# Hybrid attention and FFN kernel: the next set's row pairs in the FFN down stages turned by VectorE blocks and device memory in place of TensorE

## The reference

```python
x = x + attn_a(layernorm(x), ...)          # chunked linear attention with decay, 4 heads, chunk 128
x = x + ffn(layernorm(x), wq_gate, s_gate, wq_up, s_up, wq_down, s_down)
x = x + attn_b(layernorm(x), W_q, W_k, W_v, W_o)   # softmax attention over 1024 tokens, 1 head
x = x + ffn(layernorm(x), ...)             # the same FFN weights
# ffn: W = (wq - 128) * s[:, None];  ffn(x) = W_down(silu(W_gate x) * (W_up x)),  hidden width 1408
```

## Time and profile before

| | us |
|---|---|
| median of 3 runs | 955.58 (955.57 to 955.67) |
| the profiled execution, first to last instruction | 954.9 |

### The profile page before, as it was taken

How to read it: one execution, slowest core, us unless ns; L and a number is a source line. 1 busy time by engine, 2 the same in 40 slices (tenths; PEclk the granted TensorE clock), 3 DMA queues, 4 the chain that set the end, 5 groups by cost and what they waited for, 6 DMA issues and landing times.

```text
span 954.9 us, 13285 instructions
## 1 busy us (share of the span) xinstructions
PE 941.6 (99%) x4744; PEld 534.5 (56%) x4744; DVE 608.9 (64%) x1128; ACT 460.8 (48%) x918; POOL 478.6 (50%) x487
## 2 busy tenths in 40 slices
PE   7999999999999999999999999999999999999998
PEld 4888988888744454444544455445455444544443
DVE  7555657849677586776855466445465676766543
ACT  4443334356577545664533455323454665456631
POOL 5433424477266676666840043304333566665575
PEclk9999999999999999999999999999999999999999
DMA  9401300024200000000000000000000000110001
GB/s 324 165 11 34 133 23 23 2 89 142 95 29 1 1 1 1 1 1 1 1 1 1 1 1 1 1 1 1 1 0 1 1 0 1 45 45 1 1 23 67
DMA packets 14738, 30.31 MB, mean 32 GB/s; under 512 B 2064, under 2 KB 2128, under 8 KB 14672
## 3 DMA queue, kind: packets, MB, share of 16 engines
q1 hardware_dynamic: 14672, 29.45, 8.6%
HBM read 25.22 MB, written 4.23 MB: 31 GB/s over the span
## 4 chain that ended last, share of the span: by engine, by line
PE 93%; ACT 1%; DVE 1%; POOL 1%; DMA 1%; SPq 1%; issue 0%; POOLq 0%; DVEq 0%
PE psum L2078 54%; PE psum L2325 14%; PE psum L2327 14%; PE psum L2453 7%; PE psum L2127 2%; PE psum L2464 1%; DMA bq_col<-bq 1%; PE psum L2212 1%; PE psum L2116 1%; ACT probs L1329 0%; DVE xb_lo L1983 0%; SPq L658 0%; ACT xb_hi L1335 0%; POOL wvT_lo L922 0%; POOL wo_lo L925 0%
## 5 line engine op out<-in xcount | busy, mean ns | idle before, releaser
L872 POOL TENSOR_TENSOR hid<-hid,hid_hi 128x512 f32<-128x512 f32 x88 | 102.7, 1167 | 101.6 <-DVE hid_hi L1777 101.6
L2325 PE MATMUL psum<-xf,w_gu 128*128 128x512 f16 x352 | 133.8, 380 | 0.0
L2325 PE MATMUL psum<-xf,w_s 128*128 128x512 f16 x264 | 100.0, 379 | 0.6 <-DVE up L1750 0.4
L2327 PE MATMUL psum<-xf,w_gu 128*128 128x512 f16 x264 | 100.1, 379 | 0.0
L1191 ACT ACTIVATE hid_lo<-hid 128x512 f16<-128x512 f32 x88 | 55.0, 625 | 33.0 <-POOL hid L872 33.0
L868 POOL TENSOR_TENSOR hid<-up,gate 128x512 f32<-128x512 f32 x44 | 56.0, 1273 | 23.8 <-ACT gate L1186 23.8
L2327 PE MATMUL psum<-xq,w_s 128*128 128x512 f16 x176 | 66.7, 379 | 0.0
L2325 PEld LDWEIGHTS psum<-xf,w_gu 128*128 128x128 f16 x352 | 34.3, 98 | 53.9 <-ACT acc L1176 15.5
L1186 ACT ACTIVATE gate<-gate,sg_xs 128x512 f32<-128x512 f32 x44 | 31.7, 721 | 65.7 <-DVE gate L1760 65.7
L734 POOL TENSOR_TENSOR xrstd<-xvar,minus_half 128x1 f32<-128x1 f32 x48 | 25.5, 548 | 59.2 <-DVE xvar L1448 59.2
L1777 DVE TENSOR_SCALAR hid_hi<-hid 128x512 f16<-128x512 f32 x88 | 39.1, 444 | 19.4 <-POOL hid L868 17.9
(11 more groups left out here) (308 smaller groups left out, 2560.1 us busy)
## 6 DMA issues: line engine op xcount, KB each, us to landing
cla_wide<-cla_dram SPq DMA_DIRECT2D x16, 256.0 KB, 3.3
out<-xres SPq DMA_DIRECT2D x16, 256.0 KB, 2.0
xres<-x SPq DMA_DIRECT2D x3, 1024.0 KB, 13.3
codes_gu<-gateT SPq DMA_DIRECT2D x1, 2816.0 KB, 11.5
codes_gu<-upT SPq DMA_DIRECT2D x1, 2816.0 KB, 10.7
codes_da<-downT SPq DMA_DIRECT2D x1, 1536.0 KB, 6.8
codes_db<-downT SPq DMA_DIRECT2D x1, 1280.0 KB, 11.2
xres<-x SPq DMA_DIRECT2D x4, 256.0 KB, 3.2
```

Source lines behind the costliest of these rows:

```text
L872: nc.gpsimd.tensor_tensor(hid[:, :], hid[:, :], hid_part(hid_hi, j, half), ALU.subtract).then_inc(rest_done, 1)
L2325: nc.tensor.matmul(bank(use[0]), w, x_operand(piece, k, False), start=start and k == 0, stop=False, skip_group_check=not start)
L2327: last = nc.tensor.matmul(bank(use[0]), w, x_operand(piece, k, True), start=False, stop=k == 1, skip_group_check=not start)
```

## The change

In the down stages of blocks 0, 1 and 2 TensorE no longer turns the pairs. DVE normalises a pair into `xn` (even i) or a second buffer (odd i) and turns it in place in 32x32 blocks with one `transpose` of 128x1024 (`x_blocks`). SP writes the pair to a new device-memory tensor `blocks` by four transfers, one for each group of 32 partitions, and loads it by four more into `turned[i % 2]` in SBUF with the blocks at their turned places; each transfer consists of 1024 runs of 128 bytes. A load of pair i waits for its store, and for pairs 2 and 3 for the readers of pair i-2. ACT and POOL read `turned` in place of PSUM and `x_first`; the four copies to x_first (line 996) go. DVE's x_second reads `turned` too. `X_AFTER` becomes (3, 4, 5, 6). x_blocks of pairs 0 and 1 stand ahead of down tile 0 on DVE, those of pairs 2 and 3 after tiles 2 and 3 (`BLOCKS_AFTER`), pair 3 thus behind x_second of pair 0. In block 2 SP's stores of finished rows stand between its transfers of blocks. Banks 0, 1, 3 and 4 lose two uses each in the three stages. The turns of sets F0, B1 and F2 stay on TensorE.

```diff
--- before.py
+++ after.py
@@ -46,7 +46,13 @@
 
 X_STATS = {(0, 2): ((0,), (1,), (2, 3)), (0, 3): ((4,), (5,), (6, 7))}
 
-X_AFTER = (1, 3, 5, 6)
+X_AFTER = (3, 4, 5, 6)
+
+BLOCKS_AFTER = {2: 2, 3: 3}
+
+SQ = 32
+QUADS = P // SQ
+TURN_DMAS = 16 * QUADS
 
 
 HS = 2.0 ** -18
...
@@ -203,6 +210,9 @@
     x_last = [at(f"x_last{v}", X_TEMPS[v][2], D) for v in range(4)]
     X_PLACE = (0, 1, 1, 2, 3, 1)
 
+    xn_pair = [xn, at("xn_pair1", Z + 77824, 2 * D)]
+    turned = [at(f"turned{i}", Z + 61440 + 4096 * i, 2 * D) for i in range(2)]
+
 
     w_s = at("w_s", Z + 104448, 6 * HID, F16)
     wd_a = at("wd_a", Z + 121344, 5 * D, BF16)
@@ -254,6 +264,8 @@
 
 
     cla_dram = nc.dram_tensor("cla_dram", [4 * 4 * HEADS, P], F32, kind="Internal").ap()
+
+    blocks = nc.dram_tensor("blocks", [4 * len(MOVED), QUADS, 2 * KT, P, SQ], F32, kind="Internal").ap()
 
     psum = nc.alloc_psum_tensor("psum", [P, 8 * 512], F32)
 
...
@@ -432,10 +448,13 @@
             return "B", 0, (0, 7 + i), (1, 7 + i)
         if q == F2:
             return "B", 1, (0, 6 + i), (1, 6 + i)
-        phase, b = {F1: ("F1", 0), B0: ("F1", 1), F3: ("F2", 0)}[q]
-        if i % 2 == 0:
-            return phase, b, (0, 24 + i // 2), (1, 20 + i // 2)
-        return phase, b, (3, 12 + i // 2), (4, 10 + i // 2)
+        raise ValueError(q)
+
+    def moved_n(q, i):
+        return 4 * MOVED.index(q) + i
+
+    def moved_all(n):
+        return TURN_DMAS * (n // 2 + 1)
 
     def x_row(q, l):
 
@@ -469,6 +488,9 @@
 
     def x_2_cols(q):
         return slice(0, 4 * P) if q in (B0, B1) else slice(2 * P, 4 * P)
+
+    def x_first_of(q, i):
+        return turned[i % 2][:, 0:D] if q in MOVED else x_first[X_PLACE[q]][:, :]
 
     def x_pair(t, first, i):
         return t[:, first * GROUP:(first + 2) * GROUP].rearrange("p (k n) -> p k n", n=GROUP)[:, :, i * P:(i + 1) * P]
@@ -712,11 +734,53 @@
                 Use(sp, "mid", 0).full(v_use)
             weights(codes_da[:, :], downT[0:6 * P, :], da_in)
             weights(codes_db[:, :], downT[6 * P:JT * P, :], db_in)
-            for b in range(BATCHES):
-                for t in range(BT):
+
+            def blocks_to_dram(q, *pairs):
+
+                for i in pairs:
+                    m = moved_n(q, i)
+                    sp.wait_ge(x_blocks_done, m + 1)
+                    src = xn_pair[i % 2][:, :].rearrange("p (m j) -> p m j", j=SQ)
+                    for a in range(QUADS):
+                        sp.dma_start(blocks[m, a].rearrange("m (c i) j -> i (m c) j", c=QUADS),
+                                     src[a * SQ:(a + 1) * SQ, :, :]).then_inc(blocks_out[i % 2], 16)
+
+            def blocks_to_turned(q, *pairs):
+
+                for i in pairs:
+                    n, m = 4 * q + i, moved_n(q, i)
+                    if i < 2:
+                        phase, b = {F1: ("F1", 0), B0: ("F1", 1), F3: ("F2", 0)}[q]
+                        Use(sp, phase, b).read_out(delta(JT - 1, 1))
+                    else:
+                        sp.wait_ge(x_ab_lo, n - 1)
+                        sp.wait_ge(x_t34_done, 2 * n - 2)
+                        sp.wait_ge(x_2_lo_done, m - 1)
+                    sp.wait_ge(blocks_out[i % 2], moved_all(m))
+                    dst = turned[i % 2][:, :].rearrange("p (m a j) -> p m a j", a=QUADS, j=SQ)
+                    for a in range(QUADS):
+                        sp.dma_start(dst[:, :, a, :],
+                                     blocks[m, a].rearrange("m p j -> p m j")).then_inc(x_moved[i % 2], 16)
+
+            def store(b, *ts):
+                for t in ts:
                     sp.wait_ge(x_updated, updates(2 + b, t))
                     n = b * BT + t
                     sp.dma_start(out[n * P:(n + 1) * P, :], xres[:, n * D:(n + 1) * D]).then_inc(x_out, 16)
+
+            for q in (F1, B0):
+                blocks_to_dram(q, 0, 1)
+                blocks_to_turned(q, 0, 1)
+                blocks_to_dram(q, 2, 3)
+                blocks_to_turned(q, 2, 3)
+            blocks_to_dram(F3, 0, 1)
+            blocks_to_turned(F3, 0, 1)
+            store(0, 0, 1)
+            blocks_to_dram(F3, 2, 3)
+            store(0, 2)
+            blocks_to_turned(F3, 2, 3)
+            store(0, *range(3, BT))
+            store(1, *range(BT))
             sp.wait_ge(x_out, 4 * GT * 16)
 
 
@@ -740,15 +804,15 @@
                 pool.wait_ge(x_t2_done, n + 1)
                 if n > 0:
                     pool.wait_ge(x_34_lo, n)
-                nc.gpsimd.tensor_tensor(x_last[v][:, 0:2 * P], x_mid[v][:, 2 * P:4 * P], x_first[v][:, 0:2 * P],
+                first = x_first_of(q, i)
+                nc.gpsimd.tensor_tensor(x_last[v][:, 0:2 * P], x_mid[v][:, 2 * P:4 * P], first[:, 0:2 * P],
                                         ALU.subtract).then_inc(x_t34_done, 1)
-                nc.gpsimd.tensor_tensor(x_last[v][:, 2 * P:4 * P], x_first[v][:, 2 * P:4 * P],
+                nc.gpsimd.tensor_tensor(x_last[v][:, 2 * P:4 * P], first[:, 2 * P:4 * P],
                                         x_mid[v][:, 2 * P:4 * P], ALU.subtract).then_inc(x_t34_done, 1)
 
             def x_ab_low(q, i):
-                n, v = 4 * q + i, X_PLACE[q]
-                pool.wait_ge(x_ab_hi, n + 1)
-                nc.gpsimd.tensor_tensor(x_ab(q, i, 1), four(x_first[v][:, :]), x_ab(q, i, 0),
+                pool.wait_ge(x_ab_hi, 4 * q + i + 1)
+                nc.gpsimd.tensor_tensor(x_ab(q, i, 1), four(x_first_of(q, i)), x_ab(q, i, 0),
                                         ALU.subtract).then_inc(x_ab_lo, 1)
 
             def x_12_low(q, i):
@@ -997,8 +1061,18 @@
 
             def x_row_highs(q, i):
 
+                v = X_PLACE[q]
+                if q in MOVED:
+                    m = moved_n(q, i)
+                    act.wait_ge(x_moved[m % 2], moved_all(m))
+                    if m > 1:
+                        act.wait_ge(x_2_lo_done, m - 1)
+                    first, second = turned[m % 2][:, 0:D], turned[m % 2][:, D:2 * D]
+                    nc.scalar.activation(x_2(q, i, 0), second[:, x_2_cols(q)].rearrange("p (k n) -> p k n", n=P),
+                                         ACT.Copy).then_inc(x_b2_hi, 1)
+                    nc.scalar.activation(x_ab(q, i, 0), four(first), ACT.Copy).then_inc(x_ab_hi, 1)
+                    return
                 phase, b, first, second = x_banks(q, i)
-                v = X_PLACE[q]
                 Use(act, phase, b).full(second)
                 nc.scalar.activation(x_2(q, i, 0), bank(second[0])[:, x_2_cols(q)].rearrange("p (k n) -> p k n", n=P),
                                      ACT.Copy).then_inc(x_b2_hi, 1)
@@ -1216,7 +1290,6 @@
                                          scale=1.0 / LO).then_inc(drained[down_lo(t)[0]], 1)
                     if blk < 3 and t in X_AFTER:
                         i = X_AFTER.index(t)
-                        x_copy(NEXT_SET[blk], i)
                         if i < 3:
                             x_highs(NEXT_SET[blk], i)
                             x_34_high(NEXT_SET[blk], i)
@@ -1454,22 +1527,44 @@
                     nc.vector.tensor_scalar(cols(xn, l % 2), x_row(q, l), xmv[:, 2 * l:2 * l + 1],
                                             xrstd[:, l:l + 1], ALU.subtract, ALU.mult).then_inc(ln_xn_done, 1)
 
+            def x_blocks(q, i):
+
+                m, pair = moved_n(q, i), xn_pair[i % 2]
+                if i > 1:
+                    dve.wait_ge(blocks_out[i % 2], moved_all(m - 2))
+                elif i == 1:
+                    dve.wait_ge(hid1_lo_done, JT * (MOVED.index(q) + 1))
+                    dve.wait_ge(hid2_lo_done, JT * (MOVED.index(q) + 1))
+                for l in (2 * i, 2 * i + 1):
+                    dve.wait_ge(ln_rstd_done, ln_n("X", q, l) + 1)
+                    nc.vector.tensor_scalar(cols(pair, l % 2), x_row(q, l), xmv[:, 2 * l:2 * l + 1],
+                                            xrstd[:, l:l + 1], ALU.subtract, ALU.mult).then_inc(ln_xn_done, 1)
+                dve.wait_ge(ln_xn_done, ln_n("X", q, 2 * i + 1) + 1)
+                nc.vector.transpose(pair[:, :], pair[:, :]).then_inc(x_blocks_done, 1)
+
             def x_second(q, i):
 
-                phase, b, first, second = x_banks(q, i)
-                n, v, t = 4 * q + i, X_PLACE[q], bank(second[0])
-                Use(dve, phase, b).read_out(first)
+                n, v = 4 * q + i, X_PLACE[q]
+                if q in MOVED:
+                    m = moved_n(q, i)
+                    dve.wait_ge(x_moved[m % 2], moved_all(m))
+                    t, first = turned[m % 2][:, D:2 * D], turned[m % 2][:, 0:D]
+                    done = x_2_lo_done
+                else:
+                    phase, b, one, two = x_banks(q, i)
+                    Use(dve, phase, b).read_out(one)
+                    t, first, done = bank(two[0]), x_first[v][:, :], drained[two[0]]
                 dve.wait_ge(x_b2_hi, n + 1)
                 if n > 0:
                     dve.wait_ge(x_12_lo, n)
```

(17 more changed lines are left out.)

11 lines of the change are left out of this document (8 added, 3 removed).

## The result

The changed kernel takes 973.41 us (median of 4 runs, 971.82 to 973.73), the kernel before 955.62 beside it: a ratio of 1.0182, interval 1.0168 to 1.0197, so 17.8 us slower. The forecast was 969.0 with 950 to 1010, slower at 0.81. The profiled execution is the fastest of the four, 971.82 us with a span of 970.0; where the others spend 1.3 to 1.9 us more no profile shows.

A forecast was written before the change was run, and what follows sets the result against it. TensorE, busy 99% of the span, was taken as the bound; its 10.4 us saving would be lost behind the split's loop. Stages +10.1 and x_mid +3.3 make +13.4: 955.6 to 969.0 us, own range 956 to 980, overall 950 to 1010.

The forecast's parts named there:

- a closed loop: From DVE's yt(t) through x_mid, POOL's sums and ACT to yt(t+1): 7.1 us a tile, where TensorE needs 4.75.
- the last x_ab_low: End of a down stage: the next block's first matmul waits for it and starts 2.1 us later than before.
- the x_mid terms: DVE's x_mid, with both inputs in SBUF, lengthens: 0.4 us in each of two loops, 0.3 at the end, 3.3 in all.
- the wait for x_12_low: The next block's third product group (piece 6) waits for the last pair's x_12_low: 1.9 us more.
- the block turn: DVE's added transpose of 128x1024 f32, twelve in all: taken as 1.2 us each, far end 2.4.
- the stage's start: Two block turns and more normalisations delay yt(0) to 335.6; tile 2 needs that bank at 336.1, so covered.
- the transfers: Pairs out and in on SP's queue, 3.3 us a group of four: hidden, by about 1 us.
- The cover: Slack that hides the transfers: about 1 us, ending at about 3.75 us a group (15 ns a packet).
- rival (b): Transfers: packets over 15 ns or issue over 0.95 us; 970 to 1010 us at chance 0.14, 1035 us at 0.09.
- The rival with the slow packets: Part of (b): small packets at 27 ns, 6.9 us a group, 22 us a stage, 1035 us; chance 0.09.
- the B0 stage: Down stage before a B stage, whose queries need only the first wait: 2.1 us lost, plus 1.1 for x_mid.
- a gain of 10.4 us: TensorE's turns of 4 pairs in 3 stages removed, 0.87 us each: 945.2 us if all else kept up.

The follow-up runs named there:

- wide rows: Changed kernel with the same 96 transfers in rows of 4 KB instead of runs of 128 bytes, turn across blocks left out: 972.59 us.
- The square of experiments: Against the kernel before: only the split moved, +9.9 us; TensorE's turns dropped with SBUF reads, split as before, +7.6; both, without transfers or block turns, +17.6.

## Why the prediction was right, and where not

**Right.** The sign, and the mechanism as far as the first wait: a closed loop that is longer than TensorE's tile, the last x_ab_low (forecast 2.1 and the x_mid terms, 2.9 late; measured 2.84 and 2.90 in the F stages), the wait for x_12_low behind it (whole F stage forecast at 4.0 + 1.1 = 5.1; measured 5.13 and 5.19), the block turn (1.2; 1.25), the stage's start (covered; TensorE loses 0.2 us there at most), and the transfers (hidden; wide rows give 0.8 us, none at all and no turns 0). The cover was narrower than the 1 us forecast: DVE reaches the x_mid of pair 0 and waits 0.30 us for it. ACT waits 2.96 us for pair 0, which the prediction had given as a sign of rival (b); here the sign misleads, since the runs without that wait gain 0.8 us at most.

**Right in the sum, in part by luck: the first x_ab_low.** With the x_mid term the loop was forecast at 7.1 + 0.4 = 7.5 us; it measured 7.02 and 7.08. Against that, the y row of tile 4 was forecast at 349.5 and comes at 349.06 + 1.12 = 350.18; 0.5 us of that is already there at tile 3 (343.3, and 343.79), whose y row stands behind the turn of pair 2 on VectorE. Two loops 0.9 us short in all and a start 0.7 us late make the 2.9.

**The rival with the slow packets** was wrong. Of the rule of the Trainium skill (DMA: Bandwidth & Descriptors, Specifications) on packets under 512 B, by which it would have been 1035 us, the runs show this much: 128-byte writes to device memory land in 2.9 us where wide rows take 2.1, and eight queued loads take 0.76 us each to issue where wide ones take 0.54. A group of four was forecast at 3.3 us and takes 2.3 to 3.7. The measurement decides: slower, but far from what the rule led to.

**Mis-sized: the B0 stage.** Forecast 2.1 + 1.1 = 3.2, measured 5.6. Two things are in it. Its loop takes 7.30 and 7.33 us, which puts the first product 3.9 us late. And a term is missing altogether: after 6.9 us without work TensorE's products come 0.43 us apart, another 1.67 us. In the F stages the same fall is there, 1.3 us, under a wait for x_12_low: forecast at 1.9, it shows as 0.89 only because the slow products have used up the rest. So the F stages' sum is right, but its last term has another make-up than the forecast gave it. The three stages make 15.9 us against the 13.4 of the sum. Of the other 1.9 us to the measured 17.8, 1.6 lie between the profiled execution and the median of the four, where no profile shows them.

**Half right: the x_mid term.** I spread 0.4 us over each tile of the loop. In tiles 4 and 5 x_mid takes 0.43, not held at all; in tile 3 and behind tile 6 it is held by 0.7. Reading the half from PSUM gives about 2.2 us back, where 3.3 were forecast.

**Wrong, and hidden by the total: the bookkeeping.** The sum starts from a gain of 10.4 us that a moved split then eats. The square of experiments says otherwise. With the split left in its place there is no gain to eat: +7.6 us. A TensorE instruction is worth its time only if the split keeps up, and I took the places of before to be safe since their loop of 5.1 us stands close to TensorE's 4.75 + 0.87. But 5.1 was measured with x_mid reading PSUM. From SBUF it waits for POOL's product wherever no x_34_low has waited before it, the loop becomes 6.2 us, and the last pair's x_12_low, 0.6 us ahead of need before, becomes 2 us late; to that comes the lower clock behind TensorE's waits, which the sum doesn't have at all. Going by the parts, the move costs 10 us, and taking the turns out with the new source costs 7.6. In the forecast the move stood at 20.5 (10.4 + 10.1) and the other at a gain of 7.1 (10.4 less 3.3). One is 10.5 too much, the other 14.7 too little, and they cancel but for 4.2: that the total came near is luck to that extent.

## What to carry to other kernels

Before an operation is taken from the bounding engine, measure how far the next engines are behind it, in each place where it waits for them, and with the operands that they will then have: here the loop was 0.5 us ahead of TensorE, x_12_low 0.6 and x_ab_low 1.4. Moving an operand from PSUM to SBUF can cost a VectorE instruction more (1.07 us, 1.48 against 0.41) than the engine that filled the bank saves (0.87). The tightest spot need not be the first wait: here it was the third group of products, 1.8 us behind it. And a matching total does not show the terms right; two one-factor kernels and the one with both put each to the test.
